# Scores on the lower rows of the array beside transposed scores on the upper: an attention stage rewritten

## What is computed

```python
x = layer_norm(hidden_states, ln1_w, ln1_b)            # 16 heads of 8
q, k, v = (x @ q_w + q_b) / math.sqrt(HEAD), x @ k_w + k_b, x @ v_w + v_b
scores = jnp.einsum('bhqd,bhkd->bhqk', q, k)           # split into heads first
scores = jnp.where(causal, scores, neg)
attn = jax.nn.softmax(scores, axis=-1)
ctx = jnp.einsum('bhqk,bhkd->bhqd', attn, v)
```

## Time and profile before

| | |
|---|---|
| Median of 3 runs (lowest to highest) | 2671.97 us (2667.47 to 2672.6) |
| The profiled execution's own time; its span | 2672.96 us; 2671.2 us |
| PE, DVE, ACT, POOL busy | 1847.3, 1659.7, 949.1, 944.6 us |
| Mean granted TensorE clock | 0.839 |
| Attention stages: first piece to last context | 120.75 to 686.1 us, and 1749.8 to 2317.0 us |

### The profile page before, as it was taken

The page is one execution under the profiler, slowest core; times in us unless marked ns, Lnnn a source line. Parts: engine busy times, 40 slices in busy tenths (PEclk is TensorE's granted clock), DMA queues, the critical chain, the costliest instruction groups (busy, mean ns, idle before and its releaser), DMA issues. The chain is left out here.

```text
span 2671.2 us, 45728 instructions
## 1 busy us (share of the span) xinstructions
PE 1847.3 (69%) x10834; PEld 1034.2 (39%) x10928; DVE 1659.7 (62%) x5110; ACT 949.1 (36%) x1988; POOL 944.6 (35%) x1548
## 2 busy tenths in 40 slices
PE   3499889899710981499990075479998899840693
PEld 2133333333510770289980043223333333330472
DVE  7488778787350224867764485688887788451223
ACT  2256556566400330100000032336665566510231
POOL 4022222222445440068770563012222222337342
PEclk8689999999755995689995588679999999855797
DMA  3501111110002435000003001301011110001344
GB/s 84 212 14 26 27 27 26 25 24 6 1 25 68 124 113 146 0 0 0 0 4 36 16 16 47 106 25 26 26 25 27 27 26 14 1 4 51 109 135 128
DMA packets 109183, 120.08 MB, mean 45 GB/s; under 512 B 31264, under 2 KB 71584, under 8 KB 107936
## 3 DMA queue, kind: packets, MB, share of 16 engines
q1 hardware_dynamic: 92448, 96.50, 13.8%
q0 software_dynamic: 8192, 16.86, 1.9%
q10 hardware_dynamic: 8320, 4.19, 0.6%
HBM read 71.01 MB, written 45.71 MB: 44 GB/s over the span
## 5 line engine op out<-in xcount | busy, mean ns | idle before, releaser
L733 DVE CUSTOM_DVE_ANT_0 pA<-pA,causal 128x512 f32<-128x512 f32 (+3 forms) x1536 | 823.9, 582 | 183.0 <-PE pA L576 172.7
L777 ACT ACTIVATE wt<-pB 128x512 f32<-128x512 f32 (+3 forms) x1536 | 654.3, 496 | 442.2 <-PE pB L617 290.2
L818 POOL TENSOR_SCALAR_AFFINE_SELECT wt<-wt 128x128 f32<-128x128 f32 x1024 | 290.7, 293 | 767.6 <-ACT wt L777 746.3
L576 PE MATMUL pA<-ka,qa 125*128 125x512 bf16 (+3 forms) x1536 | 486.7, 343 | 71.1 <-PEq L272 30.0
L617 PE MATMUL pB<-qa,ka 128*128 128x512 bf16 (+3 forms) x1442 | 428.6, 333 | 51.9 <-issue 23.8
L633 PE MATMUL pC<-wt,va 128*32 128x512 f32 (+3 forms) x3072 | 347.5, 499 | 0.0
L617 PEld LDWEIGHTS pB<-qa,ka 128*128 128x128 bf16 x1536 | 145.2, 97 | 420.5 <-ACT wt L777 256.9
L576 PEld LDWEIGHTS pA<-ka,qa 125*128 125x128 bf16 x1536 | 147.5, 98 | 248.7 <-DVE mx L733 164.5
L733 DVE DVE_READ_ACCUMULATOR2_ANT mx<- 128x1 f32 x1536 | 217.0, 141 | 0.0
L1209 POOL DMA_INDIRECT y<-eo,dest x128 | 122.5, 957 | 185.3 <-issue 112.4
L1071 POOL DMA_INDIRECT xin<-keep_v,keep_send x128 | 126.9, 992 | 82.6 <-DVE keep_send L1044 43.8
(11 more groups left out here) (236 smaller groups left out, 2430.5 us busy)
## 6 DMA issues: line engine op xcount, KB each, us to landing
w<-in_L_ffn_fc_w_dram SPq DMA_DIRECT2D x64, 256.0 KB, 2.8
qa<-qk_parts SPq DMA_DIRECT2D x192, 64.0 KB
ka<-qk_parts SPq DMA_DIRECT2D x192, 64.0 KB
xi<-xin SPq DMA_DIRECT2D x32, 258.0 KB, 3.6
qk_parts<-qp SPq DMA_DIRECT2D x24, 256.0 KB, 2.4
qk_parts<-kp SPq DMA_DIRECT2D x24, 256.0 KB, 2.8
xin<-zero SPq DMA_DIRECT2D x4, 1032.0 KB, 7.1
y<-zero SPq DMA_DIRECT2D x4, 1024.0 KB, 13.1
```

Source lines behind the costliest of these rows:

```text
L576: pe.matmul(slot(s, n)[:, 0:b - a], qa[s.stage][0:MROW, h, i * P:(i + 1) * P], ka[s.stage][0:MROW, h, a:b], start=True, stop=True).then_in ...
L733: vec.tensor_tensor_reduce(out=slot(s, n)[:, 0:size], in0=slot(s, n)[:, 0:size], in1=mask, scale=1.0, scalar=LOWEST, op0=ALU.add, op1=ALU.max,
L777: act.activation(wt[g % NW][h][:, 0:e - a], pB[(g * GH + h) % NB][:, 0:e - a], ACT.Exp).then_inc(exp_done, 1)
L818: pool.affine_select(out=block_, in_=block_, compare_op=ALU.is_ge, fill=0.0, base=0, pattern=[[1, P]], channel_multiplier=-1).then_inc(mas ...
```

## The change

- `load_qk` copies the parts to rows 0 to 47 and again to rows 64 to 111: 24 DMAs a unit. Pieces use rows 0 to 47, scores rows 64 to 114, the maxima's parts stand in rows 112 to 114.
- Pieces are ordered so that each has its score's width; a piece is issued just ahead of the score with its number.
- On 32 diagonal pieces of 48, two further matmuls (128 and 64 columns, bf16 constants of 64 rows) add the causal mask into the bank. VectorE takes a plain maximum.
- `pA` has four banks, `pC` one, used by both halves in turn. The last two groups' products move into the first two groups of the next step.
- The LO split moves from VectorE to GpSimd, behind the masks of group 1; the HI split is a chain of five on VectorE after the last piece of the upper tiles. The contexts and MAX_LO come ahead of pieces 12, 16 and 20, MAX_HI ahead of piece 35 of 48.
- SP waits for the scores of the unit before, in place of its products, ahead of `load_qk`.

```diff
+HROW = P // 2
 def load_qk(sp, w, a, stage, u):
...
-        for r in range(TERMS):
+        for side in range(2):
+            for r in range(TERMS):
+                at = side * HROW + r * HD
+                sp.dma_start(dst[at:at + HD, :, :],
...
+    TILE_ORDER = (4, 5, 6, 7, 3, 0, 2, 1)
+    PIECE = [(h, i, a, min(a + HALF, (i + 1) * P)) for i in TILE_ORDER
+             for a in range(0, (i + 1) * P, HALF) for h in range(GH)]
...
-    NA, NB = 3, 3
+    NA, NB = 4, 3
...
-        pC = ps("pC", [P, SEQ])
+        pC = ps("pC", [P, HALF])
...
-                        sp.wait_ge(pv_done, s.u * NCH)
+                        sp.wait_ge(st_done, s.u * NCH)
                         load_qk(sp, w, buffers, s.shift(2).stage, s.u + 2)
...
+                    last = pe.matmul(out[:, 0:b - a], qa[s.stage][0:KROWS, h, i * P:(i + 1) * P],
+                                     ka[s.stage][0:KROWS, h, a:b], start=True, stop=not diagonal)
+                    if diagonal:
+                        for part, skip in (("lo", 0), ("hi", HROW)):
+                            last = pe.matmul(out[:, b - a - P + skip:b - a], c["pick_" + part][0:HROW, :],
+                                             c["future_" + part][0:HROW, skip:], start=False, stop=part == "hi")
+                    last.then_inc(a_done, 1)
...
+                    rows = slice(HROW, HROW + KROWS + 3)
+                    pe.matmul(pB[(g * GH + h) % NB][:, 0:e - a], ka[v.stage][rows, h, j * P:(j + 1) * P],
+                              qa[v.stage][rows, h, a:e], start=True, stop=True).then_inc(st_done, 1)
...
+                    for g in range(NG):
                         for h in range(GH):
+                            while n < len(due) and due[n] <= g * GH + h:
                                 run(s, n)
                                 n += 1
+                            scores(s, g, h)
                         if g >= LAG:
+                            products(s.shift(-1), g - LAG)
+                        elif not fixed(s, 1):
+                            products(s.shift(-2), NG + g - LAG)
...
+                            vec.reduce_max(mx[a // HALF][:, i, h:h + 1], slot(s, n)[:, 0:b - a], AX).then_inc(a_used, 1)
+                            if e == LATE - 1:
+                                split(s, event(s, n) + 1)
```

More of the change, by code:

```diff
@@ L191, in _ @@
                                           base=0, pattern=[[1, P]], channel_multiplier=-1))
[L193 to L196, removed]
+            for name, upper, lower in (("lo", -HROW, 0), ("hi", 0, HROW)):
+                pick, future = c["pick_" + name], c["future_" + name]
+                for rows, base in ((slice(0, P), upper), (slice(0, HROW), lower)):
+                    chain.link(pool.memset(pick[rows, :], 0.0))
+                    chain.link(pool.memset(future[rows, :], 0.0))
+                    chain.link(pool.affine_select(out=pick[rows, :], in_=pick[rows, :], compare_op=ALU.not_equal, fill=1.0,
+                                                  base=base, pattern=[[-1, P]], channel_multiplier=1))
+                    chain.link(pool.affine_select(out=future[rows, :], in_=future[rows, :], compare_op=ALU.is_ge,
+                                                  fill=LOWEST, base=base, pattern=[[-1, P]], channel_multiplier=1))
             pool.iota(c["rev"][:, :], pattern=[[-1, E]], base=E, channel_multiplier=0,
@@ L477, in ffn_attention @@
     MAX_LO, MAX_HI, CTX_HI, CTX_LO = "max_lo", "max_hi", "ctx_hi", "ctx_lo"
+    SPLIT_LO = 1
+    assert [b - a for h, i, a, b in PIECE] == [e - a for j, a, e in GROUP for h in range(GH)]
     def events(first, contexts):
         order = list(range(len(PIECE)))
[L481 to L485, removed]
+        order.insert(LATE + 3, MAX_HI)
+        for e, at in ((CTX_LO, 20), (MAX_LO, 16), (CTX_HI, 12)):
+            if contexts if e != MAX_LO else not first:
+                order.insert(at, e)
         return order
     ORDER = (events(True, False), events(False, False), events(False, True))
-    FINAL = [MAX_LO, CTX_HI, CTX_LO]
+    FINAL = [CTX_HI, MAX_LO, CTX_LO]
+    FINAL_AT = (12, 16, 20)
     NEV = len(ORDER[2])
-    LINKS_LO, LINKS_HI, LINKS_CTX = 3, 4, 2
-    NA, NB = 3, 3
-    LEAD = 0.6
+    LINKS_CTX = 2
+    LINKS_LO, LINKS_HI = 3, 4
+    NA, NB = 4, 3
     NW, LAG = 3, 2
-    NLINK = LINKS_LO + LINKS_HI + LINKS_CTX
     with ExitStack() as ctx:
@@ L638, in first, with step, last_b @@
                         run(s, n)
[L640 to L647, removed]
+                def step(s, due=None):
+                    events = order(s)
+                    if due is None:
+                        due = [e if isinstance(e, int) else None for e in events]
+                        for n in range(len(due) - 1, -1, -1):
+                            due[n] = due[n + 1] if due[n] is None else due[n]
+                    n = 0
+                    for g in range(NG):
                         for h in range(GH):
-                            scores(s, g, h)
-                            passed += (e - a) / GH + (behind * LEAD if h == GH - 1 else 0)
-                            while n < count and sum(share[:n + 1]) <= sum(share) * passed / total:
+                            while n < len(due) and due[n] <= g * GH + h:
                                 run(s, n)
                                 n += 1
+                            scores(s, g, h)
                         if g >= LAG:
-                            products(s, g - LAG)
-                            passed += behind * (1 - LEAD)
-                    for g in range(NG - LAG, NG):
[L658 to L665, removed]
+                            products(s.shift(-1), g - LAG)
+                        elif not fixed(s, 1):
+                            products(s.shift(-2), NG + g - LAG)
+                def last_b(s):
+                    step(s, FINAL_AT)
+                    for g in range(NG - LAG, NG):
+                        products(s.shift(-1), g)
                     for n in range(len(FINAL), len(order(s))):
@@ L672, in _ @@
             def _(vec):
[L673 to L694, removed]
                 def copy_maxima(s, n, half, unit, loaded):
@@ L714, in context, with before_unit, split @@
                                       ALU.mult).then_inc(a_used, 1)
+                def before_unit(s, back):
+                    if isinstance(s.u, int) and s.u < back:
+                        return Step(0, 0, None)
+                    return s.shift(-back)
+                def split(s, done):
+                    t = slice(HT, BT)
+                    parts = [mparts[:, t, :, r] for r in range(3)]
+                    links = s.u * LINKS_HI
+                    vec.wait_ge(a_used, done)
+                    vec.tensor_tensor(top[:, t, :], mx[0][:, t, :], mx[1][:, t, :], ALU.max).then_inc(split_hi, 1)
+                    apart(vec, split_hi, links + 1)
+                    vec.tensor_copy(parts[0], top[:, t, :]).then_inc(split_hi, 1)
+                    apart(vec, split_hi, links + 2)
+                    vec.tensor_tensor(rest[:, t, :], top[:, t, :], parts[0], ALU.subtract).then_inc(split_hi, 1)
+                    apart(vec, split_hi, links + 3)
+                    vec.tensor_copy(parts[1], rest[:, t, :]).then_inc(split_hi, 1)
+                    apart(vec, split_hi, links + 4)
+                    vec.tensor_tensor(parts[2], rest[:, t, :], parts[1], ALU.subtract).then_inc(mparts_ready, 1)
                 def step(s):
-                    n_lo = 0 if fixed(s, 0) else LINKS_LO
-                    n_ctx = 0 if fixed(s, 1) else LINKS_CTX
                     for n, e in enumerate(order(s)):
@@ L732, in step @@
                             apart(vec, a_done, event(s, n) + 1)
[L733 to L738, removed]
-                                    vec.wait_ge(a_used, before(s))
-                                split(s, 0, e, e)
@@ L806, in stage, with split @@
                                      .rearrange("p (t h r) -> p t h r", t=BT, h=GH)).then_inc(v_staged[s.stage], 1)
+                def split(s):
+                    t = slice(0, HT)
+                    parts = [mparts[:, t, :, r] for r in range(3)]
+                    links = s.u * LINKS_LO - LINKS_LO
+                    apart(pool, a_used, before(s))
+                    pool.tensor_copy(parts[0], mx[0][:, t, :]).then_inc(split_lo, 1)
+                    apart(pool, split_lo, links + 1)
+                    pool.tensor_tensor(rest[:, t, :], mx[0][:, t, :], parts[0], ALU.subtract).then_inc(split_lo, 1)
+                    apart(pool, split_lo, links + 2)
+                    pool.tensor_copy(parts[1], rest[:, t, :]).then_inc(split_lo, 1)
+                    apart(pool, split_lo, links + 3)
+                    pool.tensor_tensor(parts[2], rest[:, t, :], parts[1], ALU.subtract).then_inc(mparts_ready, 1)
                 def first(s):
@@ L810, in first, with step @@
                         stage(s.shift(d))
-                def mask(s):
```

(13 more changed lines are left out.)

88 lines of the change are left out of this document (36 added, 52 removed).

## The result

2654.01 us, median of 20 runs (2633.89 to 2676.37), against 2679.09 for the kernel before: ratio 0.9915, 95% interval 0.9891 to 0.9938. The sign was right; about 25 us came where 97 were forecast.

The account below looks back on a forecast made before the run. It took TensorE's order to bound the kernel, at 33.8 us a step. From 2673 us it took 153 for the steps, added 53 for loads and 2 for unit 0: 2575 us, range 2510 to 2665.

Parts of the forecast that it names:

- the halves overlap: Attention steps: scores and transposed scores on the two row halves stream together fully, saving TensorE 7.65 us a step.
- TensorE's 27.1: TensorE's time per attention step after the change: 23.1 us of streaming plus 4 us of restarts.
- VectorE as the bound: Attention step: VectorE's floor of 26.8 us (25.5 to 28.2), busy over 90% of a step.
- masks hidden behind it: Mask matmuls on TensorE: 2.55 us a step at the upper bound, which was taken; free at the lower.
- low maxima late behind the queued loads: Before group 8 of a step, TensorE waits about 1 us for low maxima queued behind 24 loads.
- That makes 28.3: Attention step: VectorE's floor of 26.8 us plus 1.5 us of stalls.
- 28.7: Forecast attention step in us, with low maxima about 1 us late; from 27 to 31.5, against 33.8 before.
- The loop turns, 4 us each, stay in both: Where the loop of three attention steps turns: 4 us extra each, the same in both kernels.
- 153 were forecast: Attention steps: 15 in each of two layers, 30 x (33.8 - 28.7) us saved.
- Twice 26.5 = 53: Projection ahead of attention, both layers: 36 added loads put 26.5 us each on the path; 0 at the lower end.
- the clock falls: Rival: attention steps drop to the 1.2 GHz level, +427 us, about 3100 us; chance 4%.
- Not side by side: Rival: score halves do not stream together, TensorE takes 34.7 us a step, kernel 2755 us; chance 14%.

Follow-up runs that it names:

- run 10: The kernel of run 7 with each maximum taken over the first half of its piece's columns only: 2474.98 us, ratio 0.9256 to the kernel before.
- run 9: The kernel of run 7 without the mask matmuls: 2533.00 us, ratio 0.9473 to the kernel before.
- run 2: The changed kernel with all attention steps written out, no loop of three: 2543.67 us, ratio 0.9522 to the kernel before.
- written-out kernel: The changed kernel with its attention steps written out instead of looped (run 2): 2543.67 us; with upper copies loaded behind the low maxima (run 7): 2515.24 us.
- run 1: The changed kernel measured again, unchanged: 2639.52 us, ratio 0.9882 to the kernel before.
- run 4: The changed kernel with the transposes of the high maxima seven pieces behind the last late piece instead of three: 2656.42 us, ratio 0.9924 to the kernel before.
- run 7: The kernel of run 2 with each unit's upper copy issued behind the low maxima instead of ahead of them: 2515.24 us, ratio 0.9390 to the kernel before.
- run 5: The changed kernel with scores and transposed scores both on array rows 0 to 63: 2937.17 us, median of 4.

## Why the prediction was wrong

Held by the runs: the halves overlap (0.22 us a pair); TensorE's 27.1 (26.7 written out, run 10); VectorE as the bound, masks hidden behind it (run 9); reductions of 512 columns 0.60 apart; low maxima late behind the queued loads, once steps are short (run 2).

**The step that failed is "That makes 28.3", and 28.7 from it.** It is a sum of durations and stalls, and meets the written-out kernel's step (28.05), in part by luck: VectorE is busy 25.3 us there, not 26.8, and idle 2.8, not 1.5. It was then subtracted from 33.8, a time measured in a loop that holds 1.9 us of the loop's own work (31.9 without). The changed kernel pays 2.1 us as well (30.1 against 28.05), and the sum had no term for it: in the loop VectorE idles 4.4 us a step. Which of the loop's instructions take it was not separated.

**"The loop turns, 4 us each, stay in both"** failed as well: 6.6 us each now (37.35 less 30.7), with the clock at 1.2 GHz for 10 us behind the stop, not 3. Clock that falls inside steps makes another 0.6 us (30.7 on average against 30.1). Counted from the first link of VectorE's high split to the next, which takes in all 30 steps, they gave 80 us where 153 were forecast. The 24 without a turn gave 85, 3.5 each in place of 5.1. The six with a turn, where 31 were forecast, took 5 more than before. So of the 73 us missing, half lie in plain steps and half in turns and the clock around them.

**"Twice 26.5 = 53"** was 44 in the first execution and 48 in that of run 1: right in kind and nearly in size, but not a fixed price a layer.

Of the rivals, *the clock falls* was in part true at 0.94. *Not side by side* had its mechanism excluded, and its size: at full clock that step is 31.0 written out, not 34.7. That the wait for high maxima could be taken out was my own later error (run 4): VectorE needs the time anyway. The median of the twenty lies 20 us above the profiled execution, and no trace shows these 20 us. The projection's wait, which differs by 11 and 7 us between two executions of equal length, may be one source of the wider spread; it was not tested.

## What to carry to other kernels

A step summed from instruction durations may only be set against one with the same surcharge: a loop's own instructions cost 2 us of every step here, on both sides or on neither. What a change takes from the bound engine makes each fixed stop (a turn, a queued DMA) dearer, so look for these before the engines' sums. Small transfers that someone waits for go ahead of bulk loads on their queue: that was worth 35 us (run 7).

## What the runs showed of the hardware

How long TensorE stayed at 1.2 GHz behind a stop differed with its matmuls: 3 us with 125 to 128 rows, 10 with pairs of 48 and 51, and 115 at least with these one at a time on one half (run 5, 396.51 to 511.57), while it was shown busy throughout. That the rows are the cause was not tested by itself. The Trainium skill (TensorE: Matmul & The Clock Gate, "HAM oscillation — how this bites in real kernels") tells of waits between groups that bring the clock down again and again; runs 2 and 7 agree: 0.89 to 0.94 in the ten steps with waits of 1.20 us and more, and 1.00 once the waits are gone. Taking work off TensorE (the masks, run 9) made the kernel 22 us longer, 6 of them shown in the attention steps.
